# Local attention: probabilities scaled by GpSimd ahead of the transposes, and a new order of TensorE's work

## The reference, cut to what matters

```
h = shift_token(x)
q, k, v = split(h @ wqkv, 3)                  # 8 heads of 64
q = l2norm(q) * qs;  k = l2norm(k) * ksc
q, k = rotary_xpos(q, k)
# each window of 128 queries sees the 128 keys of its own and of the window before
sim = einsum('bhwid,bhwjd->bhwij', 8 * bq, bk), masked
attn = softmax(sim)
o = einsum('bhwij,bhwjd->bhwid', attn, bv)
x = x + o @ wo
```

## Time and profile before

| | |
|---|---|
| median of 3 runs | 3784.04 us (3783.09 to 3787.71) |
| profiled execution | 3784.49 us, its span 3782.6 us |
| TensorE busy | 3587.0 us, 95% of the span |
| VectorE busy | 2511.2 us, 66% |
| ScalarE busy | 1607.4 us, 42% |
| GpSimd busy | 1407.7 us, 37% |
| mean granted clock of TensorE | 0.990 of full speed |
| first attention stage | from 2290.08 us of the span |

### The profile page before, as it was taken

The page is one execution under the profiler, slowest core; times in us unless marked ns, Lnnn a source line. Parts: engine busy times, 40 slices in busy tenths (PEclk is TensorE's granted clock), DMA queues, the critical chain, the costliest instruction groups (busy, mean ns, idle before and its releaser), DMA issues. The chain is left out here.

```text
span 3782.6 us, 59344 instructions
## 1 busy us (share of the span) xinstructions
PE 3587.0 (95%) x21704; PEld 2541.9 (67%) x21704; DVE 2511.2 (66%) x5351; ACT 1607.4 (42%) x3142; POOL 1407.7 (37%) x1569
## 2 busy tenths in 40 slices
PE   7888888887999999999999998999999999999999
PEld 5666666666555888888887665666656566666565
DVE  8999999998665555555554446777743367777432
ACT  5878777774001222222222214666631156666211
POOL 6888888885000000000001223444421134444111
PEclk9999999999999999999999999999999999999999
DMA  1000000002111000001001211111111111121121
GB/s 41 1 12 12 12 12 12 1 7 68 53 34 45 11 11 13 11 11 35 11 11 52 71 64 59 38 37 57 35 60 50 37 59 35 34 72 33 45 67 39
DMA packets 150758, 129.33 MB, mean 34 GB/s; under 512 B 20852, under 2 KB 147592, under 8 KB 150472
## 3 DMA queue, kind: packets, MB, share of 16 engines
q1 hardware_dynamic: 150472, 125.54, 10.7%
HBM read 87.73 MB, written 37.77 MB: 33 GB/s over the span
## 5 line engine op out<-in xcount | busy, mean ns | idle before, releaser
L420 POOL TENSOR_TENSOR ssm_acc<-ssm_acc,ssm_weighted 128x512 f32<-128x512 f32 x255 | 338.3, 1335 | 108.6 <-ACT ssm_weighted L565 108.4
L406 POOL TENSOR_SCALAR ssm_ub<-ssm_uT,ssm_bcT 128x512 f32<-128x512 f32 x512 | 360.1, 725 | 24.1 <-PE ssm_pu L1106 20.3
L1106 PEld LDWEIGHTS ssm_pu<-ident,ssm_ub 128*128 128x128 f32 x2048 | 238.4, 142 | 184.3 <-issue 84.9
L1106 PE MATMUL ssm_pu<-ident,ssm_ub 128*128 128x128 f32 x2048 | 309.5, 279 | 50.7 <-DVE ssm_state L779 33.4
L3073 PE MATMUL win_pa<-win_w_wqkv,tile_hT 128*128 128x512 f32 x744 | 343.6, 598 | 0.0
L1122 PE MATMUL ssm_pt<-ident,ssm_state 128*128 128x128 f32 x2040 | 280.9, 279 | 57.2 <-DVE ssm_acc L789 29.3
L2506 PE MATMUL glu_up<-block_hT,glu_w_w 128*128 128x512 f32 x704 | 308.2, 596 | 8.0 <-DVEq L82 8.0
L779 DVE TENSOR_TENSOR_SCAN ssm_state<-ssm_da,ssm_carry,ssm_pu 128x512 f32<-128x512 f32 x256 | 312.6, 1262 | 1.8 <-issue 1.8
L2844 POOL TENSOR_TENSOR block_hT<-tile_straight,tile_turned 128x512 f32<-128x512 f32 x124 | 158.2, 1276 | 402.9 <-DVE tile_turned L2951 402.8
L779 DVE TENSOR_TENSOR_SCAN ssm_state<-ssm_da,ssm_pu 128x512 f32<-128x512 f32 x256 | 296.8, 1200 | 8.4 <-PE ssm_pt L1122 5.7
L553 ACT ACTIVATE ssm_da<-ssm_dt,ssm_decay 128x1024 f32<-128x1024 f32 x256 | 294.4, 1151 | 0.7 <-DVE ssm_dt L857 0.6
(11 more groups left out here) (368 smaller groups left out, 7468.2 us busy)
## 6 DMA issues: line engine op xcount, KB each, us to landing
x<-block_y SPq DMA_DIRECT2D x16, 512.0 KB, 2.9
block_add<-x SPq DMA_DIRECT2D x16, 512.0 KB, 5.7
tile_raw<-in_tables SPq DMA_DIRECT2D x64, 128.0 KB, 2.2
a<-tile_y SPq DMA_DIRECT2D x64, 128.0 KB, 1.7
block_xs<-a SPq DMA_DIRECT2D x32, 256.0 KB, 3.3
block_x<-a SPq DMA_DIRECT2D x16, 512.0 KB, 5.0
x<-block_half_y SPq DMA_DIRECT2D x16, 256.0 KB, 2.1
block_x<-x SPq DMA_DIRECT2D x8, 512.0 KB, 3.9
```

The source lines that it names most:

```text
L406: nc.gpsimd.tensor_scalar(ub[:, i % 2, t, :], uT[:, k % 2, t, :], bcT[:, k % 2, t, n:n + 1], 1.0, ALU.mult, ALU.mult).then_inc(ub_ready.se ...
L420: nc.gpsimd.tensor_tensor(acc[:, k % 2, t, :], acc[:, k % 2, t, :], weighted[:, j, :], ALU.add)\
L1106: last = nc.tensor.transpose(pu[c][:, t * P:(t + 1) * P], ub[:, i % 2, t, c * P:(c + 1) * P], ident)
```

## The change

GpSimd multiplies each head's 128x256 probabilities by the reciprocal of its denominator, after the exponentials and before TensorE transposes them. The widening, its transposes, their copy and VectorE's multiply go; what is left of the last is a copy. Reciprocals are taken for four heads at a time. The clamp and the power for keys and for queries are split (`norms`), and the squares of the keys are summed before the second maxima, those of the queries behind them. The second half of the probabilities is transposed in the next tile's body, all weighted sums of a tile run together there, the output projection goes to the end of the body, and the transposes of the input are done two tiles ahead. Values get a third buffer. The stores and residuals come a tile later. The diff, cut to the lists of each engine and the new functions:

```diff
-        wide, rden_rows = s.sb("wide", [P, INNER]), s.sb("rden_rows", [P, PR, P])
+        third = s.sb("third", [P, H2, DH])
+        v_of = [v[:, 0, :, :], third[:, :, :], v[:, 1, :, :]]
...
         @block.sync
-                if before:
-                    sp.wait_ge(y_ready.sem, y_ready.at(turn.i - 1))
-                    store(turn.before())
-                    if more:
-                        start_residual(turn.next())
+                if turn.i >= 2:
+                    sp.wait_ge(y_ready.sem, y_ready.at(turn.i - 2))
+                    store(Turn(turn.pair - 1, turn.side))
+                    start_residual(turn)
...
         @block.gpsimd
+            def norms(turn, j):
+                pool.wait_ge(ss_steps.sem, ss_steps.at(turn.i, 2 - j))
+                nc.gpsimd.tensor_scalar(ss_kept[:, j, :], ss[:, j, :], 1e-24, None, ALU.max).then_inc(kept_ready.sem, 1)
+                pool.wait_ge(kept_ready.sem, kept_ready.at(turn.i, 2 - j))
+                nc.gpsimd.tensor_tensor(rn[:, turn.side, j, :], ss_kept[:, j, :], minus_half[:, j, :], ALU.pow).then_inc(rn_ready.sem, 1)
+
+            def scale(turn, g):
+                pool.wait_ge(rden_ready.sem, rden_ready.at(turn.i, g + 1))
+                for j in range(2):
+                    for r in range(2):
+                        head = 4 * g + 2 * r + j
+                        nc.gpsimd.tensor_scalar(probs[:, head, :], probs[:, head, :], rden[:, head:head + 1], 1.0,
+                                                ALU.mult, ALU.mult).then_inc(scaled.sem, 1)
...
                 if more:
                     rotation(turn.next())
+                scale(turn, 0)
+                if more:
+                    norms(turn.next(), 1)
+                    norms(turn.next(), 0)
+                scale(turn, 1)
...
         @block.scalar
                     values(turn)
-                if more:
-                    hidden(turn.next())
-                if before:
-                    reciprocal_rows(turn.before())
                 exps(turn, 0, 0)
                 exps(turn, 0, 1)
                 if more:
                     square(turn.next(), 0)
+                if before:
+                    columns(turn.before(), 1)
+                if more:
                     square(turn.next(), 1)
-                columns(turn, 0)
                 exps(turn, 1, 0)
                 exps(turn, 1, 1)
-                columns(turn, 1)
-                widen(turn)
+                columns(turn, 0)
+                if more2:
+                    hidden(Turn(turn.pair + 1, turn.side))
                 if more:
                     queries(turn.next())
...
         @block.vector
                 maxima(turn, 0)
-                if before:
-                    output(turn.before())
                 if more:
                     rotate(turn.next(), 0)
                     rotate(turn.next(), 1)
...
+                reciprocals(turn, 0)
+                if before:
+                    columns(turn.before(), 1)
+                if turn.i >= 2:
+                    residual(Turn(turn.pair - 1, turn.side))
+                if more:
+                    square_sums(turn.next(), 1)
                 maxima(turn, 1)
                 if more:
                     square_sums(turn.next(), 0)
-                    square_sums(turn.next(), 1)
-                columns(turn, 0)
                 if before:
-                    residual(turn.before())
-                dve.wait_ge(exp_ready.sem, exp_ready.at(turn.i))
-                nc.vector.reciprocal(rden[:, :], den[:, :]).then_inc(rden_ready.sem, 1)
+                    output(turn.before())
                 if more:
                     unit_keys(turn.next())
-                columns(turn, 1)
+                columns(turn, 0)
+                reciprocals(turn, 1)
                 if more:
                     keys(turn.next())
...
         @block.tensor
-                if more:
-                    transposes(turn.next())
                 scores(turn, 0)
-                if before:
-                    spread_reciprocals(turn.before(), True)
                 if more:
                     project(turn.next(), 0)
                     project(turn.next(), 1)
...
+                if before:
+                    columns(turn.before(), 1)
                 scores(turn, 1)
-                columns(turn, 0)
+                if before:
+                    weighted(turn.before())
                 if more:
                     project(turn.next(), 2)
-                if before:
-                    output(turn.before(), turn.next() if more else None)
-                columns(turn, 1)
-                weighted(turn, 0)
+                columns(turn, 0)
+                if more2:
+                    transposes(Turn(turn.pair + 1, turn.side))
                 if more:
                     heads_to_rows(turn.next(), turn)
-                weighted(turn, 1)
+                if before:
+                    output(turn.before(), Turn(turn.pair + 1, turn.side) if more2 else None)
...
+            columns(Turn(NT // 2 - 1, 1), 1)
+            weighted(Turn(NT // 2 - 1, 1))
             output(Turn(NT // 2 - 1, 1), None)
```

More of the change, by code:

```diff
@@ L2825, in _ @@
             trailing(sp, body)
-            sp.wait_ge(y_ready.sem, y_ready.at(NT - 1))
-            store(Turn(NT // 2 - 1, 1))
+            for side in range(2):
+                sp.wait_ge(y_ready.sem, y_ready.at(NT - 2 + side))
+                store(Turn(NT // 2 - 1, side))
         @block.gpsimd
         def _(pool):
-            give_credit(pool, sum_ready, rn_ready)
+            give_credit(pool, sum_ready, rn_ready, scaled)
             give_turn(pool, table_ready, table_ready, sum_ready, kept_ready, rn_ready)
@@ L3043, in _ @@
             trailing(dve, body)
+            columns(Turn(NT // 2 - 1, 1), 1)
+            residual(Turn(NT // 2 - 1, 0))
             output(Turn(NT // 2 - 1, 1))
@@ L3048, in _ @@
         def _(pe):
-            give_credit(pe, qkt_ready)
+            give_credit(pe, qkt_ready, pt_ready)
             give_turn(pe, tp_ready, proj_ready, qkt_ready)
```

97 lines of the change are left out of this document (42 added, 55 removed).

## The result

The changed kernel takes 3792.53 us (median of 20 runs, 3788.14 to 3795.65), the kernel before 3785.56 us beside it (20 runs, 3781.39 to 3789.04). The ratio is 1.0018, 95% interval 1.0011 to 1.0024: a loss of some 7 us where I forecast a gain of 9.8. It is just under the 0.2% that the prediction set as its bound for a measurable change, but its interval leaves out 1. The profiled execution took 3795.59 us, its span is 3793.7.

What follows compares the result with a forecast made beforehand. TensorE was busy 95%, but a VectorE and GpSimd chain was taken to set the tile. 2 × (30 × (15.05 − 15.23) + 0.5) = −9.8 us from 3784.49 gave 3774.7, less 0.45 gave 3774.2; range 3764 to 3800.

Steps and rivals of the forecast that it cites:

- The chains: In the steady tile, rotation, key sum, multiplies, power and odd copy lead to key transposes at 8.03; query transposes at 7.5.
- the two waits besides: TensorE waits before the weighted sums (about 0.2 us) and at the key and query transposes, roughly 0.9 us a tile together.
- The size of the steady gain: Each steady tile takes 15.05 us against 15.23, 0.18 less.
- step 6: From the key transposes to the end of the next projections TensorE needs 7.00 us, with the projections at 3.60.
- step 4: On GpSimd, clamp to the power's start takes 0.34 us and the first power 1.64, ending at 6.54.
- Ends of a stage: The first tile takes 0.6 us less and the last 1.1 more, net +0.5 us a stage.
- A: GpSimd's multiplies are dearer and the change loses: gain gone at 0.50 us each, 3797 us at 0.55; chance 0.19.
- B: No measurable change, 3777 to 3791 us, centre 3780: one or two hand-offs are 0.1 us longer; chance 0.31.
- C: The chains are shorter and TensorE's own 14.2 us a tile is the limit, about 3722 us; chance 0.04.
- The weighed rule: VectorE reading two SBUF inputs contends with GpSimd over shared interfaces; the first bias was charged its long 0.35 us.
- The other reading: Four 128x512 multiplies beside VectorE operations took 15% more; if all four here paid that, 0.27 us a tile.

Runs made afterwards that it cites:

- The half-width: The kernel after with the first four GpSimd multiplies over 128 of the 256 columns only; steady tile 14.83 us, program 3775.0 us.
- the ends mended: The kernel after with matmuls in the first tile's waits, the next stage's power moved earlier and the last reciprocal ahead of the copy; 3785.06 us, ratio 0.9993.

## Why the prediction was wrong

The direction was wrong: a gain of 9.8 us was forecast, and the kernel became 7 us slower. The time of 3792.5 lies inside the range of 3764 to 3800. By its own steps:

**The chains: right.** Rotation, key sum and multiplies came out to 0.01 (4.57 against 4.56), the period is set where the prediction put it, and the two waits besides (0.28 before the weighted sums, 0.41 before the keys with 0.28 before the queries; some 0.97 together against "roughly 0.9") are where it put them, though the query transposes came at 7.25 and not 7.5. The half-width and the extra multiply moved the period as that chain says. One reading was off without consequence: ahead of the widening ScalarE has no wait in the trace of before, only ahead of the row copy.

**The size of the steady gain: 0.06, not 0.18.** Three terms were too small: in step 6 the projections, now directly behind scores, 3.70 in place of 3.60 (+0.10); in step 4 the hand-off from the multiplies over the clamp to the power, 0.41 in place of 0.34 (+0.07), and the power, 1.67 in place of 1.64 (+0.03). Half of the pair's 3.27 was too little for the first one: the two overlap in the trace, and the first alone took 1.67 in the kernel before as well. The 0.07 is the step from the last multiply to the clamp, 0.08, which the sum left out. Other terms take 0.08 back, 0.05 of it in step 6, and 0.02 because the sum of 15.03 was taken as 15.05. The 0.1 for a change of grouping was known to the prediction; it counted three changes fewer in TensorE's work, which is not the bound, and did not see that one of those left, between scores and projections, now stands inside the cycle that sets the period. With the ends mended and the steady tile as it is, the ratio was 0.9993 [0.9984, 1.0002], an interval that includes no change at all; and in the profiled execution the early clock of the first tile makes 1.4 us a stage of the gain.

**The failed step: "Ends of a stage".** With the second and the second-last tile at −0.18 it gave +0.1 us a stage for these four tiles; measured is 2.51 + 2.31 + 2.28 − 0.06 = +7.0. Over two stages of the profiled executions the sum was off by 20 us: 14 are these tiles, and 7 are the 56 steady ones at 0.12 each. Without the 14 the sum of the tiles would have been a small gain. Some 8 of the 14 hang on the clock, which was low in both second and both last tiles of this execution and need not be so in another; the medians, 17 us from the forecast, hold a mixture. The step missed three things.
- The second tile was taken as steady, and the first as cold as before. The waits that the new order lays bare in the first tile are followed by the low clock in the second, for 2.5 us. Filled, they are not.
- For GpSimd the prediction weighed only the tile's own work. The next stage's power stands in the same list, behind the new multiplies: 2.3 us, of which moving the call gave back 2.0. By the trace of before it started in good time, 0.74 of idle on VectorE; nothing in the forecast asked what comes behind the second multiplies at tile 29.
- The last tile cost 2.3, not 1.1. At the full clock it is 18.54, 0.75 more than before, so that the forecast's 1.1 was rather high. The other 1.53 come with the lower clock, and 0.86 of them through one order: slow transposes hold up a copy, and the reciprocal stands behind it.

**The rivals.** A, a dearer multiply, did not come: 0.46 against its parity at 0.50. B is nearest by size: its band is no change within 0.2%, and the ratio is 1.0018 (3792.5 itself is past its 3791, but the kernel before also took 1.5 us more in these runs, 3785.56, than the 3784.04 that the band was set by). Partly it is so by reason: hand-offs and a group were 0.2 longer together. The larger part, the ends, stood in no rival. C came no nearer than the best variant, 14.88, where VectorE's unbroken run is the limit and not TensorE's 14.2.

**The weighed rule.** The contention that the prediction charged is there beside the multiplies too, but it depends on the moment. In the steady tile of the kernel after, the first bias took 0.15 in place of the charged 0.35, because it starts at 2470.36, only 0.11 before the third multiply ends. Where more of a multiply was left, it took until that multiply's end, to within 0.02 us: 0.32 to 0.37 in five tiles of the kernel after, 0.34 in the steady tile of the kernel with the clamps on VectorE, and 0.45, for the second bias, beside the extra multiply:

```profile
2475.93 0.50 POOL L2865 TENSOR_SCALAR win_spare<-win_c_masks,win_rden 128x256 f32<-128x256 f32 x1
...
2475.98 0.45 DVE L2989 SCALAR_TENSOR_TENSOR win_nbias<-win_highest,tile_rn 128x2 f32<-128x2 f32 x1
```

Beside GpSimd's power it is hardly held, 0.16 to 0.19 with over 1 us of the power left. The other reading, 15% on each of four multiplies in the earlier trace rows, was an average over unlike ones: the first three took 0.70 each, and the last, beside the VectorE operation of the earlier trace rows, took 1.13:

```profile
406.85 1.13 POOL L406 TENSOR_SCALAR ssm_ub<-ssm_uT,ssm_bcT 128x512 f32<-128x512 f32 x1
```

Beside the tiny bias no multiply was stretched: all took 0.47 to 0.50. What the Trainium skill, page "GPSIMD Engine Reference", section "Key points", says of interfaces shared with VectorE when it reads two SBUF inputs agrees with both, the bias of 0.45 and the multiply of 1.13.

**What remains open.** Which condition decides whether the clock falls is not settled: the same program shows both forms of the second tile and of the last. That the waits precede it and that filling them was followed by the full clock in 10 of 10 stages is shown for the second tile; for the last one, where 15 of 24 unfilled stages have the full clock anyway, not even that. No run moved the multiplies against the bias alone, so what the contention costs a tile is not measured by itself.

A version that beats both kernels came out of the experiments: clamp on VectorE, ends mended, residual later, 3768.15 us, 0.9945 of the kernel before. Of its 20 us, 2 × 28 × 0.15 = 8 come with the clamp's place and 2 × 28 × 0.14 = 8 with the residual's, neither of which is part of the change, and 2 × 28 × 0.06 = 3 from the change's steady tile. Whether such moves would help the old order as well was not tried.

## What to carry to other kernels

A change that saves a tenth in a steady tile is decided at the ends of its loop. Write out the first two and the last two iterations as carefully as the steady one, with every call of other stages that stands in the same engine's list. When work leaves TensorE and a wait takes its place, ask of that wait what clock the next group will run at. And when a group changes its neighbour, its own busy time can change: price it from a row with the same neighbour. The same holds for a small operation beside another engine's long one: its price depends on how much of the long one is left.

## What the runs showed of the hardware

- The price of a change from a group of 64 rows or columns to a full one falls on the group behind: 3.70 in place of 3.60 for the eight projections, 1.98 in place of 1.88 for the four behind weighted sums, and 3.60 again for the projections with one transpose between.
- TensorE's low clock comes and goes between two passes through the same code in one execution: with the filled last wait the second tile took 17.60 us in one stage and 15.16 in the other, and with the earlier last reciprocal the weighted sums of the last tile took 1.97 in one and 3.32 in the other.
- GpSimd's multiply of fp32 by a column takes 0.355 us at 128 columns and 0.46 at 256.
- VectorE's 128x2 bias with two SBUF inputs takes 0.15 us alone. Started while one of GpSimd's multiplies or sums had over 0.2 us left, it took until that one ended (0.27 to 0.34 for 60 of them in the kernel with the clamps on VectorE, 0.35 for 62 in the kernel before); beside the power it took 0.16 to 0.19. The other way round, a 128x512 multiply took 1.13 in place of 0.70 beside a VectorE operation on two SBUF tensors of 128x512.
- An fp32 matmul with 128 columns of weights and 512 moving columns, put into a wait, took 0.91 us in a run of three, and each shows as two records in the trace.
